# A fused decoder layer on one core: self maxima and self residual rows moved one search round later on VectorE

## The reference

```
x = x + self_attention(layernorm(x))         # q, k layer-normed per head, causal mask, softmax
x = x + cross_attention(layernorm(x), ctx)   # softmax over the 32 largest scores of each row only
x = x + ffn(layernorm(x))                    # ternary weights, activations rounded to 8 bits,
                                             # silu(gate) * up, amax of the product per row, down
```

## Time and profile before

| what | value |
|---|---|
| time, median of 3 runs (lowest, highest) | 3911.12 us (3903.92, 3913.15) |
| the profiled execution: its own time, its span | 3917.24 us, 3915.5 us |
| busy: PE, DVE, ACT, POOL | 3310.2, 3220.0, 2451.7, 1917.9 us |
| mean granted TensorE clock | 0.867 of full speed |

### The profile page before, as it was taken

The page is one execution under the profiler, slowest core; times in us unless marked ns, Lnnn a source line. Parts: engine busy times, 40 slices in busy tenths (PEclk is TensorE's granted clock), DMA queues, the critical chain, the costliest instruction groups (busy, mean ns, idle before and its releaser), DMA issues.

```text
span 3915.5 us, 61337 instructions
## 1 busy us (share of the span) xinstructions
PE 3310.2 (85%) x18502; PEld 2433.7 (62%) x18502; DVE 3220.0 (82%) x7571; ACT 2451.7 (63%) x4921; POOL 1917.9 (49%) x2444
## 2 busy tenths in 40 slices
PE   1577888999989998999999989999899988877765
PEld 1355567766666676667667667667666766554542
DVE  4311189999989999899989998999989998999961
ACT  2344466676777677667766677767666776555533
POOL 0122334446555466546654655546554654355445
PEclk7677878898999989988989999988998898887768
DMA  8112232232223222322223222322233221211100
GB/s 279 46 49 65 80 84 73 74 82 75 51 76 88 75 69 79 84 79 74 76 72 84 75 52 74 87 76 67 79 88 83 65 71 41 62 46 36 33 22 19
DMA packets 167443, 283.04 MB, mean 72 GB/s; under 512 B 40639, under 2 KB 52939, under 8 KB 166606
## 3 DMA queue, kind: packets, MB, share of 16 engines
q1 hardware_dynamic: 160782, 275.98, 25.9%
q10 hardware_dynamic: 6336, 3.15, 0.3%
HBM read 113.27 MB, written 31.46 MB: 37 GB/s over the span
## 4 chain that ended last, share of the span: by engine, by line
DVE 33%; PE 32%; POOL 11%; issue 8%; ACT 6%; SPq 4%; DMA 1%; DVEq 0%; POOLq 0%; ACTq 0%
DVE cW L881 15%; DVE top L876 12%; PE bank L682 6%; PE bank L607 6%; PE bank L654 5%; SPq L513 4%; PE bank L593 3%; PE bank L670 2%; PE bank L701 2%; PE bank L635 2%; POOL hh L1111 2%; POOL srs L1147 2%; POOL hh L1115 2%; PE bank L694 2%; DVE smx L1013 2%
## 5 line engine op out<-in xcount | busy, mean ns | idle before, releaser
L881 DVE MATCH_REPLACE8 cW<-top,cW 128x512 f32<-128x512 f32 x1536 | 1026.3, 676 | 0.0
L876 DVE MAX8 top<-cW 128x8 f32<-128x512 f32 x1536 | 980.7, 680 | 0.0
L1168 POOL TENSOR_TENSOR cS<-cS,cW 128x512 f32<-128x512 f32 x512 | 642.2, 1276 | 233.2 <-ACT cW L825 232.7
L797 ACT ACTIVATE PT<-bank 128x512 f32<-128x512 f32 (+3 forms) x1024 | 538.0, 525 | 314.4 <-PE bank L593 310.6
L607 PE MATMUL bank<-cv,PT 128*128 128x33 f32 x4096 | 586.0, 290 | 121.8 <-ACT PT L797 120.6
L607 PEld LDWEIGHTS bank<-cv,PT 128*128 128x128 f32 x4096 | 555.0, 210 | 157.0 <-ACT PT L797 151.0
L1175 POOL TENSOR_SCALAR cnb<-top 128x2 f32<-128x2 f32 x256 | 49.3, 193 | 871.6 <-DVE top L876 857.9
L607 PEld LDWEIGHTS bank<-sv,PT 128*128 128x128 f32 x2560 | 398.7, 211 | 77.7 <-ACT PT L797 55.4
L825 ACT ACTIVATE cW<-cW,cnb 128x512 f32<-128x512 f32 x512 | 347.8, 734 | 127.6 <-DVE cW L881 127.2
L819 ACT ACTIVATE cS<-cS,cnb 128x512 f32<-128x512 f32 x512 | 380.1, 742 | 46.9 <-POOL cnb L1175 24.0
L682 PE MATMUL bank<-w_group,xT 128*128 128x384 f32 x1024 | 403.3, 541 | 0.0
(11 more groups left out here) (151 smaller groups left out, 6131.8 us busy)
## 6 DMA issues: line engine op xcount, KB each, us to landing
sk_stack<-part SPq DMA_DIRECT2D x512, 64.0 KB, 2.0
sq_stack<-part SPq DMA_DIRECT2D x512, 64.0 KB, 2.0
ck_stack<-part SPq DMA_DIRECT2D x512, 64.0 KB, 2.0
cq_stack<-part SPq DMA_DIRECT2D x512, 64.0 KB, 2.0
w_group<-wa_by_group SPq DMA_DIRECT2D x32, 768.0 KB, 4.8
w_group<-wc_by_group SPq DMA_DIRECT2D x32, 768.0 KB, 4.3
feed<-in_x SPq DMA_DIRECT2D x32, 256.0 KB, 3.0
feed<-in_ctx SPq DMA_DIRECT2D x32, 256.0 KB, 3.0
```

Source lines behind the costliest of these rows:

```text
L797: act.activation(PT[k][:, 0:n], turned_ps[k][:, 0:n], ACT.Copy).then_inc(turned_read, step("turned_read", label))
L876: dve.max(top8[:, j, r, :], src[:]).then_inc(topk, step("topk", (c, r, "max", j)))
L881: dve.match_replace(cW[j][:], top8[:, j, r, :], src[:], REPLACED).then_inc(topk, step("topk", (c, r, "replace", j)))
L1168: pool.tensor_tensor(cS[m % 2][j][:], cS[m % 2][j][:], cW[j][:], ALU.subtract).then_inc(cprob, step("cprob", (m, j)))
```

## The change

Four moves in fixed lists; no instruction is added or taken away.

- DVE: `self_maxima(s-1, 1)` comes after `ROUND_1` of half 0 where it came before it.
- DVE: `self_maxima(s, 0)` and `self_rows(s)` come after `ROUND_1` of half 1 where they came before it.
- POOL: `silu(s-1, late)` comes before `self_bias(s-1, 1)` where it came after it.
- ACT: the order of exponentials in cells 1 to 3 changes from self 2 | self 3, cross 0 | cross 1 to cross 0 | cross 1, self 2 | self 3.

```diff
@@ ScalarE, exponentials(s, k)
                         elif k == 1:
+                            cross_exp(c, 0)
+                        elif k == 2:
+                            cross_exp(c, 1)
                             self_exp(s - 1, 2)
-                        elif k == 2:
+                        elif k == 3:
                             self_exp(s - 1, 3)
-                            cross_exp(c, 0)
-                        elif k == 3:
-                            cross_exp(c, 1)
@@ VectorE, loop over slots
                         top(c, 0, FIRST_MAX)
+                        top(c, 0, ROUND_1)
                         self_maxima(s - 1, 1)
-                        top(c, 0, ROUND_1)
                         sum_squares(s)
...
                         top(c, 1, FIRST_MAX)
+                        top(c, 1, ROUND_1)
                         self_maxima(s, 0)
                         self_rows(s)
-                        top(c, 1, ROUND_1)
                         feed_stats_of(s + 1)
@@ GpSimd, loop over slots
                         cross_bias(c, 0)
+                        silu(s - 1, False)
                         self_bias(s - 1, 1)
-                        silu(s - 1, False)
```

## The result

| | before | after |
|---|---|---|
| time, median of 6 runs each (lowest, highest) | 3907.52 us (3891.5, 3913.15) | 3939.65 us (3933.72, 3954.8) |
| the profiled execution: own time, span | 3917.24, 3915.5 us | 3934.83, 3933.0 us |
| mean granted TensorE clock | 0.867 | 0.865 |

The ratio after to before is 1.0097, with a 95% interval of 1.0067 to 1.0126. It is a ratio of means, and the medians give 1.0082. It rests on six runs of each kernel. The prediction was 3914 us with a range up to 3934. It was wrong, also in its sign.

A forecast was written before the change was run, and what follows sets the result against it. No single engine was taken as the bound: DVE and PE hand the path to each other, with POOL between. The terms summed to +2.9 us, so 3920.1 for the profiled execution and 3914 for the median, range 3888 to 3934.

The forecast's parts named there:

- part 2: Self residual rows, slots 14 to 1: covered DVE waits partly kept; -10.7 and -5.9 over five batches, -2.6 in the first.
- part 5: POOL's run in slots 9 and 10 starts 2.51 us later, +15.1; later `cnb` in slot 2 delays slot 3, +3.
- part 4: Early MLP chunk: new DVE waits of 1.26 us in slots 5, 8 and 12, slot 8's free; +15.1 over six batches.
- part 6: The rest, such as moved exponentials, later transposes and the drain: costed at nothing; PE's lower clock noted without a row.
- part 3: Late MLP chunk: DVE's 0.56 us idle goes, counted in slots 7, 12 and about half in 13; -8.6 over six batches.
- Part 1: First searches, slot 20: ROUND_1 fills 2.51 us of DVE's 5.25 us wait, then no wait until slot 30; -2.5, once.
- rival A: PE, full in slots 0 and 1, takes back the gains of slots 14 and 15; 3931 us, chance 0.23.

The follow-up runs named there:

- half0_only: Kernel before with only the first half of DVE's move (half 0) plus POOL's and ACT's new orders; 3917.06 us, ratio 1.0013.
- half1_only: Kernel before with only the self maxima of heads 0 and 1 and the self residual rows after ROUND_1 of half 1; 3934.43 us, ratio 1.0064.
- rows_only: Kernel before with only the self residual rows moved after ROUND_1 of half 1; 3909.23 us, ratio 0.9991.
- experiment 2: Changed kernel with the self maxima of heads 0 and 1 back before ROUND_1 of half 1, rows still late; 3894.03 us, ratio 0.9965.
- silu_first: Changed kernel with POOL's early-chunk silu moved ahead of self_bias(s, 0); 3893.32 us, ratio 0.996.

## Why the prediction was wrong, by its own steps

**The miss in sum.** The forecast has +0.9 us a batch over the five full ones, and the traces have +4.0. Slots 14 and 15 give 3.2 where part 2 had 2.1. Slot 1 is 1.2 us longer where it had 1.2 shorter, slots 3 and 4 are 1.6 longer where part 5 had 0.6, and slot 5 is 2.2 longer where part 4 had 1.26. The other slots, 8 and 9 taken as a pair, are within about 0.2. Two steps failed. Part 2, with part 5's price for slot 3, has DVE keep what it hands back at its next meetings with PE; this is what the two traces differ by. And part 6 left PE's clock at nothing, with parts 3 and 4 stopping at DVE. That step doesn't show between these two traces, but it does between the experiments, where the same edit costs 25 or 46 us and the difference stands in slot 14.

**Part 1 right in sum, by luck.** It said that DVE has no wait until slot 30. There is one of 1.18 us still in slot 20, before the self maxima of the second half. In `half0_only` the first wait falls by 2.52 us, the second grows to 3.78, and slot 20 is not shorter at all. `half1_only` makes it 2.3 us shorter, and both halves together 4.8. At slot 22 the kernel after is 3.4 us ahead (having come to slot 20 1.0 us later); 2.5 was forecast. With the first batch's share of part 2 it was 7.0 us ahead at slot 37 (5.1 forecast).

**Part 2 failed.** The step was "So PE itself can use 2.3 of the 2.51". It read PE's wait for `so` as PE's only tie in slot 15. ACT, busy without a pause from the end of slot 14, copies `part` only 0.9 us sooner after `xres` (15.52 us against 16.39), and PE's next unit needs it. PE's gain is 0.8 us. I looked at who ended the wait, not at who would end the next one. The same part called the 1.17 us of slot 1 "the last wait of this run" and passed over the 2.18 us that DVE waits before `rr` in that slot. PE is full there, and in all twelve traces with late rows that wait is 4.70 to 4.72, so the 2.51 won in slot 14 is waited off. (The trace names no releaser for it; `rr` reads a bank that PE writes.) What is left goes in slot 3 and in slot 5, where a wait of 0.94 us for PE's projection before `x2t` is new. Alone the rows' move is worth nothing: `rows_only` has 0.0 us a batch. With part 2 at nothing the forecast's own terms give +4.2 us a batch, and the trace has +4.0. This is in the main rival A's mechanism, with ACT beside PE, and its mark ("longer by 3 is A"). Its 3931 us for the median is about 3937 for the profiled execution, which took 3934.83.

That near match is partly luck, since part 2 isn't at nothing in every company. On top of the first half the rows' move is worth 0.48% (experiment 2). The loss in slot 3 comes once: 1.9 us with POOL's later `cnb`, 1.5 with the late rows, and 1.9 with both. So the rows hand it back only where the first half hasn't lost it already. A sum of separately priced moves can't show that.

**Part 3 right in its waits, blind to slots 14 and 3.** The late waits of 0.56 us went, other than in slot 10. Slots 7, 12 and 13 of `half0_only` are 0.7, 0.7 and 0.3 us shorter, 1.7 a batch where 1.4 was forecast. Slot 14 gains another 2.6 there, behind a shorter low stretch of slot 13, and slots 3 to 5, 11 and 15 lose more than that. The batch is 0.7 us shorter in that trace.

**Part 4 right in its mechanism, blind to what hangs on it.** The new waits are 1.20 us, in slots 5, 8 and 12, and slot 8's is taken back in slot 9 (+1.2, -1.3). But the forecast's part 3 and part 4 both stopped at DVE. What DVE's last `hmx` of slot 12 gains or loses moves POOL's `inner_quant` of slot 13, PE's wait for it, and the clock behind that. Moving the late chunk forward alone cut the wait to 1.1 us in three of five batches and slot 14 by 2.6 us on average (`half0_only`). With the early chunk's delay beside it the three slots 14 with a wait of 4.6 us are long again (33.8). The two errors cancel in the traces' sum against before, and show only when one of them is undone: 31 to 39 us came back for the three slots where 15.1 was the price.

**Part 5 right in slot 10, low in slot 3.** Slot 10 lost 2.3 us (forecast 2.51), and the late wait of 2.85 (forecast 2.9) came. ACT's wait for `cnb` came to 3.60 us and not to 5.9, since ACT was later too. In slot 2 `cnb` comes 1.93 us later, and the `x2t` wait of slot 3 is 4.67 us, both as forecast. Its price was not: 1.9 us a slot where the sum had 0.6. It can't be split, since slot 3 is longer by 1.9 in `half0_only`, which has POOL's later `cnb` alone, by 1.5 in `rows_only`, which has not, and by 1.9 with both. Behind `x2t` PE waits too, and behind PE's wait stands the low clock (slot 3 after, timeline, then its window):

```profile
1722.02 0.69 DVE L924 TENSOR_TENSOR x2t<-bank,x1res 128x512 f32<-128x512 f32 x1 [4.67 <-issue]
1722.77 1.11 PE L705 MATMUL bank<-ident,sx 128*128 128x128 f32 x4 [3.38 <-DVE x2t L924]
```

```profile
1709.56:1738.53 28.97, 25.26 (x111) 20.18 (x111) 24.20 (x57) 18.26 (x34) 10.32 (x16) 0.62 0.51 129
```

The slot's granted clock before was 0.75, in its window:

```profile
1704.36:1731.42 27.06, 21.02 (x108) 15.14 (x109) 24.20 (x57) 18.02 (x34) 10.33 (x16) 0.75 0.45 118
```

Matmul for matmul the work is the same, 111 against 108, and PE is busy with it 4.2 us longer. I had seen the start of this (the matmuls of 5.84 us in the earlier trace rows) and written that the cost stands in no row. It could have been bounded from the windows.

**Part 6 left the clock at nothing.** From slot 37 to 117 the low stretches add up to 334.5 us before and 368.6 after, 34.1 us more. Slots 3 alone have more than that, 45.9 us (12.8 to 22.0 each on average), and the other slots together 11.8 us less. A microsecond at half the clock is half a microsecond of matmuls lost, so 17 us is the most that this can be of the 19.9 lost there. It is an upper bound and no term of its own: in `rows_only` the low time grew by 23.9 us and the time by 0.0, because PE had the room. Where PE is the late engine, the factor of a half holds. From PE's unit in slot 13 to DVE's `xres` in slot 14 it is 1588.84 - 1551.59 = 37.25 us before, with 6.8 low, and 1595.32 - 1555.69 = 39.63 after, with 11.6 low. Less half of the low time both are 33.8. The Trainium skill prices it in the same way (TensorE: Matmul & The Clock Gate, Terms: the penalty is the throttled time times one less the ratio of the clocks), and this stretch agrees.

**What stays open.** The medians lie 32 us apart and the two traces 17.6. Against the later runs of the kernel before the medians lie 27 to 30 apart. The traces' part is placed slot by slot above; which slots hold the rest, no trace shows. ACT's new order and POOL's silu were never run apart from the first half of DVE's move, so `half0_only` prices the three together. The batches after differ among each other (430 and 423 us) with the same instructions, and why two of them lack the wait in slot 13 is not settled. The low stretches of slots 11 and 15 shift between batches and kernels (slot 11 takes 27.0 to 31.0 us), and no experiment explained them.

## What to carry to other kernels

A wait on the busiest engine is worth closing only if the next meeting of the engines isn't already set by a third one: ask of each wait who would end it if its releaser were early. Price moves together and not one by one: here one of them was worth nothing alone and 0.48% beside another. What stands behind a tiny instruction in an in-order list moves with it; here a bias of 0.19 us held back the MLP's product, and the repair was to swap the two. When an edit lengthens a wait of TensorE, price the matmuls behind it at the lower clock too, and follow the wait one slot further than the engine on which the edit was made.

## What the runs showed that was not expected

- The length of slot 14 goes step by step with the low stretch in slot 13. Over the full batches of the eight traces with late self rows and no filler, 40 in all, it is 27.9 to 29.3 us behind a stretch of 0, 29.4 behind 3.4, 31.6 to 31.7 behind 6.8, 32.1 to 32.8 behind 10.2 and 33.7 to 33.8 behind 13.7.
- Sixteen matmuls whose result is thrown away, put where PE waits, brought the ratio from 1.0097 to 1.002 (18 us by the medians). The same filler in front of other waits (slots 7 and 10) brought nothing that could be told.
- The mean clock hardly shows it: 0.867 before, 0.865 after, 0.865 again in `silu_first`, which by the ratios is 1.4% faster. It is where the low stretch falls that counts, and not only how much of it there is. In `silu_first` the low time from slot 37 to 117 is 30.7 us above that of before, and yet these slots take 14.1 us less.
